# The first pair of heads in a cross-attention kernel: its key rotation on VectorE, its queries in a bank of their own, weights rounded in another order

## What is computed

```python
lat = layer_norm(latents, ln_lat_g, ln_lat_b)
ctx = layer_norm(context, ln_ctx_g, ln_ctx_b)
q = (lat @ Wq).reshape(b, n, HEADS, DHEAD).transpose(0, 2, 1, 3)
kv = ctx @ Wkv
k, v = jnp.split(kv, 2, axis=-1)
...
k = apply_rope(k, cos[None, None], sin[None, None])   # [x1*cos - x2*sin, x2*cos + x1*sin]
attn = jnp.einsum('bhnd,bhsd->bhns', q, k) * scale
attn = jnp.clip(attn, -11.0, 11.0)
attn = jax.nn.softmax(attn, axis=-1)
out = jnp.einsum('bhns,bhsd->bhnd', attn, v)
```

## Time and profile before

| what | us |
|---|---|
| median of 3 runs | 314.24 |
| all three runs | 313.40, 314.24, 314.36 |
| the profiled execution, its time | 312.95 |
| the profiled execution, its span in the trace | 311.2 |

### The profile page before, as it was taken

How to read it: one execution, slowest core, us unless ns; L and a number is a source line. 1 busy time by engine, 2 the same in 40 slices (tenths; PEclk the granted TensorE clock), 3 DMA queues, 4 the chain that set the end, 5 groups by cost and what they waited for, 6 DMA issues and landing times.

```text
span 311.2 us, 6616 instructions
## 1 busy us (share of the span) xinstructions
PE 292.3 (94%) x2482; PEld 204.0 (66%) x2482; DVE 243.4 (78%) x449; ACT 162.7 (52%) x326; POOL 209.0 (67%) x208
## 2 busy tenths in 40 slices
PE   7898999999999999999999999999999999899983
PEld 6776576666668666666687676556686665476651
DVE  3985998875875849899787798977847699687856
ACT  3446466667443734774426465774436368314741
POOL 6446775665573838686737578498827597968764
PEclk9999999999999999999999999999999999999999
DMA  7554412211210201111201111111101200000001
GB/s 218 179 151 114 123 38 57 62 36 44 60 28 9 52 17 36 35 36 36 51 19 34 37 34 36 33 38 34 36 0 37 53 1 2 0 19 0 1 2 34
DMA packets 16319, 14.24 MB, mean 46 GB/s; under 512 B 4832, under 2 KB 11808, under 8 KB 16288
## 3 DMA queue, kind: packets, MB, share of 16 engines
q1 hardware_dynamic: 14992, 13.49, 16.6%
q10 hardware_dynamic: 1296, 0.33, 0.5%
HBM read 4.89 MB, written 0.52 MB: 17 GB/s over the span
## 4 chain that ended last, share of the span: by engine, by line
PE 52%; DVE 21%; POOL 9%; issue 8%; ACT 5%; SPq 3%; DMA 2%; POOLq 0%; ACTq 0%; DVEq 0%
PE pv L645 10%; PE sc L631 9%; PE sums L666 6%; PE pj_k L569 4%; PE side L751 4%; DVE ks L1286 3%; PE pj_k L571 3%; PE pj_k L570 3%; SPq L536 3%; POOL moe L1868 3%; POOL e L1806 3%; PE side L827 2%; DVE ksin L1350 2%; DMA kswap<-ksin 2%; DVE kcos L1350 2%
## 5 line engine op out<-in xcount | busy, mean ns | idle before, releaser
L1806 POOL TENSOR_SCALAR e<-e 128x1024 f32<-128x1024 f32 x64 | 71.6, 1119 | 60.7 <-ACT e L944 47.6
L944 ACT ACTIVATE e<-sc 128x1024 f32<-128x1024 f32 x64 | 65.6, 1024 | 28.1 <-PE sc L631 28.0
L631 PEld LDWEIGHTS sc<-qs,ks 64*128 64x128 f32 x768 | 49.6, 185 | 21.7 <-issue 18.5
L645 PE MATMUL pv<-e,v 128*64 128x256 f32 x512 | 62.3, 385 | 1.6 <-POOL e L1806 0.8
L631 PE MATMUL sc<-qs,ks 64*128 64x256 f32 x768 | 62.5, 295 | 0.4 <-ACT e L944 0.2
L1799 POOL TENSOR_TENSOR krot<-kcos,kswap 128x512 f32<-128x512 f32 x32 | 45.2, 1411 | 9.8 <-DMA kswap<-ksin 7.0
L645 PEld LDWEIGHTS pv<-e,v 128*64 128x64 f32 x512 | 34.1, 136 | 24.2 <-issue 7.2
L952 ACT ACTIVATE u<-pv 128x256 f32<-128x256 f32 x32 | 12.3, 386 | 62.2 <-PE pv L645 55.5
L1286 DVE TENSOR_TENSOR ks<-krot,ks 128x512 fp32r<-128x512 f32 x32 | 33.6, 1051 | 0.1
L1350 DVE TENSOR_TENSOR ksin<-pj_k,sinT 128x512 f32<-128x512 f32 x32 | 21.9, 685 | 3.4 <-PE pj_k L571 3.2
L936 ACT ACTIVATE v<-pj_k 128x512 f32<-128x512 f32 x28 | 16.8, 598 | 14.3 <-PE pj_k L571 13.9
(11 more groups left out here) (289 smaller groups left out, 560.4 us busy)
## 6 DMA issues: line engine op xcount, KB each, us to landing
kswap<-ksin SPq DMA_DIRECT2D x126, 64.0 KB, 2.0
ctx_in<-in_ctx_dram SPq DMA_DIRECT2D x4, 256.0 KB, 3.4
prod<-in_L_xattn_Wkv_dram SPq DMA_DIRECT2D x2, 512.0 KB, 6.0
x_in<-in_x_dram SPq DMA_DIRECT2D x1, 512.0 KB, 6.0
prod<-in_L_xattn_Wq_dram SPq DMA_DIRECT2D x1, 512.0 KB, 6.8
wo<-in_L_xattn_Wo_dram SPq DMA_DIRECT2D x1, 512.0 KB, 4.4
fwe<-in_L_ffn_We_dram SPq DMA_DIRECT2D x1, 512.0 KB, 4.4
out_dram<-x_in SPq DMA_DIRECT2D x3, 128.0 KB, 1.8
```

The source lines that it names most:

```text
L631: last = nc.tensor.matmul(sc[:, h, c * NT:(c + 1) * NT], ks[rows, j % 3, k_part, chunk], qs[rows, j % 2, q_part, :], start=(k_part + q_par ...
L645: last = nc.tensor.matmul(pv_bank[DH * h:DH * h + DH, 0:NT], v[:, c, col:col + DH], e[:, j % 3, h, c, :], start=(c == 0), stop=(c == SC - 1))
L944: nc.scalar.activation(e[:, j % 3, :, 2 * half:2 * half + 2, :].rearrange("p h c n -> p h (c n)"), sc[:, :, :], ACT.Exp, scale=SCALE).then ...
L1806: nc.gpsimd.tensor_scalar(a, a, EXP_HIGH, EXP_LOW, ALU.min, ALU.max).then_inc(s_clip, 1)
```

## The change

- VectorE instead of POOL adds `krot` of pair 0, right behind the split of the transposed tokens.
- The products of pair 1 move behind that: its sines after `krot` of pair 0, its cosines after `key_lo(0)` and `query_lo(0)`.
- The queries of pair 0 go into the PSUM bank `own_bank`, and no longer take a place in `PROJECTIONS`; the places of all behind them shift by one.
- ACT rounds `wq` before it issues its two swaps, and `wv` after the transposed tokens (before: `wv`, swaps, `wq`, tokens). POOL's rest of `wv` now waits for `key_lo(0)`.
- POOL's second `affine_select` moves behind the two 1/sqrt of the start.
- ACT's `key_hi(1)` moves from slot -1 into slot 0, between the value copies and the second exponential. POOL's first clip of slot 0 moves ahead of `rotate(2)`.
- Eight `keep_busy` matmuls fewer: 5 instead of 10 ahead of the transposed tokens, 3 instead of 6 ahead of the first queries.

```diff
-WARM_UP = {"cos_T": 11, "ctx_T": 0, "sin_T": 4, "lat_T": 10, "queries": 6, "scores": 6}
+WARM_UP = {"cos_T": 11, "ctx_T": 0, "sin_T": 4, "lat_T": 5, "queries": 3, "scores": 6}
...
-        if 0 <= slot + 1 < NPAIR:
+        if 1 <= slot + 1 < NPAIR:
             units.append(("queries", slot + 1))
...
         def query_bank(j):
-            return pj_k[PLACE["queries", j] % 2]
+            return pj_k[PLACE["queries", j] % 2] if j else own_bank
...
                 if j == 0:
                     pe.wait_ge(s_wq, 1)
-                bank_free("queries", j)
+                else:
+                    bank_free("queries", j)
...
-            act.wait_ge(ld["wv"], 16)
-            nc.scalar.activation(wvS[:, 0, :], wv_in, ACT.Copy).then_inc(s_wvhi, 1)
+            act.wait_ge(ld["wq"], 16)
+            nc.scalar.activation(wqS[:, 0, :], wq_in, ACT.Copy).then_inc(s_wqhi, 1)
 
             act.wait_ge(s_kmul, 1)
             for r in (2, 3):
                 to, at = HALF * r, HALF * (r ^ 1)
                 act.dma_start(kswap[to:to + HALF, 0, :], ksin[at:at + HALF, 0, :]).then_inc(s_kswap[0], 16)
-            act.wait_ge(ld["wq"], 16)
-            nc.scalar.activation(wqS[:, 0, :], wq_in, ACT.Copy).then_inc(s_wqhi, 1)
             take("lat_T", 0)
+            act.wait_ge(ld["wv"], 16)
+            nc.scalar.activation(wvS[:, 0, :], wv_in, ACT.Copy).then_inc(s_wvhi, 1)
...
                     value_copy(1)
+                    key_hi(1)
...
-                if 0 <= slot + KV_AHEAD < NPAIR:
+
+                if 0 <= slot + KV_AHEAD < NPAIR and slot + KV_AHEAD != 1:
                     key_hi(slot + KV_AHEAD)
...
-            def key_products(j):
+            def key_products(j, which=(0, 1)):
...
-                for dst, trig in ((ksin, sinT), (kcos, cosT)):
+                for i in which:
+                    dst, trig = ((ksin, sinT), (kcos, cosT))[i]
...
             key_products(0)
-            key_products(1)
             tokens_normalise(0)
             dve.wait_ge(s_wqhi, 1)
             split_lo(wqS[:, 1, :], wq_in, wqS[:, 0, :]).then_inc(s_wq, 1)
             split_latT(0)
+
+            dve.wait_ge(s_kmul, 2)
+            dve.wait_ge(s_kswap[0], 64)
+            nc.vector.tensor_tensor(krot[:, 0, :], kcos[:, 0, :], kswap[:, 0, :], ALU.add).then_inc(s_krot, 1)
+            key_products(1, (0,))
             key_lo(0)
             query_lo(0)
+            key_products(1, (1,))
...
+            ctx_rstd(0)
+            tokens_rstd(0)
             nc.gpsimd.affine_select(out=sp_v, in_=sp_v, compare_op=ALU.not_equal, fill=-1.0, base=-1,
...
-            ctx_rstd(0)
-            tokens_rstd(0)
-
+
+
+            pool.wait_ge(s_klo, 1)
             pool.wait_ge(s_wvhi, 1)
             nc.gpsimd.tensor_tensor(wvS[:, 1, :], wv_in, f(wvS[:, 0, :]), ALU.subtract).then_inc(s_wv, 1)
...
-                if 0 <= slot + KV_AHEAD < NPAIR:
+
+                if slot == 0:
+                    clip(slot, 0)
+                if 1 <= slot + KV_AHEAD < NPAIR:
                     rotate(slot + KV_AHEAD)
                 second_layer(slot, -1)
-                if 0 <= slot < NPAIR:
+                if 1 <= slot < NPAIR:
                     clip(slot, 0)
```

## The result

The changed kernel takes 315.82 us (median of 15 runs, 314.12 to 317.24), the kernel before beside it 313.74 (15 runs): ratio 1.0057, 95% interval 1.0038 to 1.0075. It is slower by 0.6%, where no change was forecast, and it lies outside the range. The profiled execution took 316.20 us, its span is 314.4 (before: 311.2); the two traces differ by 3.2 us where the medians differ by 2.1. Medians are over all runs, while a ratio compares the means of the fast ones (without 317.30 and 317.65 of e2 and 543.88 of e7), so it need not equal the ratio of the medians.

A forecast was written before the change was run, and what follows sets the result against it. PE's losses in the first 40 us were taken to bound the kernel; 2.04 us at the scores, 0.6 left at the clips, summed to 0.45 off the median 314.24, 313.8 us, range 312.1 to 314.7.

The forecast's parts named there:

- The entry: Sums of pair 1, at 36.17, wait for VectorE's additions; what the sums win is what the kernel wins.
- Tokens and first keys: Stretch from `lat` to the first scores: scores at 18.19, 2.04 us earlier.
- The mechanism: SP's queue: later sines of pair 1 delay its swap, so the swap of pair 2 starts at 21.73 instead of 20.71.
- and from there to POOL's start 2.14: From the last issue of pair 2's swap to POOL's `krot` of pair 2: 2.14 us, as in the trace.
- rival 1: SP's queue does not stall again, swaps of pairs 2 and 3 come 0.74 earlier: 313.1 us, chance 0.25.
- rival 3: Swaps of pairs 2 and 3 land late, 3.5 instead of about 2.1: slower, 315.6 us, chance 0.15.
- some 2 us: PE's wait ahead of the first product with values, which starts near 28.9; a sign that the forecast is right.
- The `affine_select` beside `lat`: POOL beside VectorE: `lat` ends at 13.86 if held, about 13.5 if free; the middle, 13.68, was taken.
- Covered, as said: PE has 1.4 us to spare ahead of the first product with values; smaller delays ahead of it are hidden.
- the scores' lead: PE's first scores of pair 0 come 2.04 us earlier, at 18.19 instead of 20.23.
- the 0.6 us that were left at the clips: POOL's clips of pair 0 end at 28.85 instead of 29.46, leaving 0.6 of the 2.04 us.

The follow-up runs named there:

- e2: Changed kernel with the swap of pair 2 ahead of the context of batch 2 and the loads in SP's queue: 315.07 us, ratio 1.0021.
- e7: e3 with `krot` of pair 0 back on POOL: 311.76 us, ratio 0.9939.
- e3: Changed kernel with both products of pair 1 early again, ahead of `lat`: 311.68 us, ratio 0.9948.
- e6: Changed kernel with POOL's second `affine_select` back ahead of the two 1/sqrt: 314.85 us, ratio 1.0021.
- e5: Changed kernel with 10 unread matmuls in PE's wait ahead of the first product with values: 313.30 us, ratio 1.0006.
- e9: Kernel before with one edit, POOL's first clip of pair 0 ahead of `krot` of pair 2: 312.38 us, ratio 0.9958.
- e4: Kernel before with only both products of pair 1 moved behind the split of the transposed tokens: 317.72 us, ratio 1.0148.
- e10: e7 with the first clip of pair 0 behind `krot` of pair 2 again: 313.91 us, ratio 1.0007.

## Why the prediction was wrong

**Right.** *The entry.* What the sums of pair 1 lose is what the kernel loses; 275 us behind them hold in all 13 traces. *Tokens and first keys.* Scores at 18.58 against 18.19: `krot` on VectorE took 0.68 (0.69 taken), `ks` 0.69, and 0.37 of the difference is there already when the swap of pair 1 is issued (17.34 against 16.97), of which most is the later start. *The mechanism.* The later sines hold up the swap of pair 1, SP's loads slip with it, and the swap of pair 2 stands right behind the context's load, later than before.

**The step that failed is a term of the sum: "and from there to POOL's start 2.14".** The working had put `krot` of pair 2 at 26.44; it started at 28.49, 2.05 later, in three pieces. 0.37 is the difference above. From the first issue of pair 1's swap to the last of pair 2's it was 25.06 - 17.34 = 7.72 instead of 4.76 + 2.57 = 7.33, so 0.39: the long issue left the swap, as rival 1 had it, but went to `wo` (1.74 us), which stands in the same queue, and nothing was gained. The largest piece, 1.29, is the landing: from the last issue to POOL 3.43 (28.49 - 25.06) instead of 2.14. The swap's landing had been carried over from a place where the last load was issued 2.35 us ahead of it (18.36 to 20.71) to one where it is 0.12 ahead.

The last DMA of the swap took 3.3 us instead of 2.0 to land. No run changes the landing alone: e2 takes the loads away and meets another wait.

**What happened is nearest to rival 3**, which had a chance of 0.15. Its landing of 3.5 us is what the trace shows (3.3 to 3.8), its clips at 30.63 ended at 30.88, and its time of 315.6 was measured as 315.82. The prediction had named the loads that stand closer and the landing from which the case decides, 2.6 us, and still took the 2.14 us of a swap that follows them at a distance. The 3.5 of the earlier trace rows was luck: it belongs to the swap issued at 244.9 us, with no load in front of it. Rows for a better chance were there in the swap of pair 2 itself: in the kernel before its first two DMAs, 2.35 and 2.91 us behind the last load, took 2.7 and 2.8 us, its last two 2.0.

The Trainium skill has a rule that should have raised that chance: "DMA: Bandwidth & Descriptors", section "Queues, rings and completion order", says that on each DMA engine descriptors are consumed in the order of their ring, and that the write which counts up the semaphore lands only after every earlier write of that engine. The traces agree: behind loads issued 0.12, 1.18 and 2.35 us ahead the swap of pair 2 landed in 3.4, 2.9 and 2.4 us (medians of four, changed kernel, e3, before), and 2.0 with the loads behind it (e2).

**A step was missing altogether: the clock.** The prediction let PE wait "some 2 us" ahead of the product with values and priced the wait alone. The clock fell in it, and that cost another 1.2 to 1.7 us (e6, e5). Its working held none of this, and so the nearness of rival 3 to the measured time is in part luck: it put VectorE's `ks` last, and in the trace the sums follow PE without a wait; and it adds 1.33 us to a median of 314.24, where the measured rise is 2.08 from 313.74.

**Weighed wrongly.** The `affine_select` beside `lat`: the middle of held and free was taken. `lat` was held: it ended at 14.17, 0.32 behind the `affine_select` (13.85), as it had ended 0.34 behind `wvS`. So the Trainium skill's rule, "SBUF — State Buffer", section "SBUF: two separate sides", held here for a tensor-scalar operation too. By e6 its price is 0.30 us in `lat`, of which 0.16 reaches the swap.

**Covered, as said.** The rest of `wv` behind the keys (`wvS` at 18.18, 2.39 us), the own bank and the fewer unread matmuls cost nothing that can be seen. What the working did not separate is which edit wins: it credited the scores' lead with the 0.6 us that were left at the clips. In e9 the clip in POOL's idle time is worth 1.8 us by itself (1.3 by the ratio) with scores no earlier than before (20.26), and e7 shows no loss from scores 0.44 us later than in e3: the lead is worth nothing that can be measured.

## What to carry to other kernels

A duration read for a transfer belongs to what stands in front of it in its queue: when a change pushes loads closer to a small transfer on the path, take the landing from rows with as many bytes in front and as little time between, not the median. Closeness alone misleads, as the swap of pair 3 shows (0.10 us behind 132 KB, landed in 2.0). Where an estimate leaves PE waiting for about 2 us, read the granted clock behind waits of that length before pricing the wait alone. A change of many edits is best told apart by what each does to the one wait that binds: here one clip moved into idle time was the gain, and one pair's products moved out of their place cost more than twice as much.

## What the runs showed of the hardware

PE's waits of 1.87, 2.14 and 2.45 us ahead of the first product with values (e4, e6, changed kernel) each went with a fall of the clock to 0.50 (1.2 GHz); behind those of 0.84 and 1.35 us (before, e10) it stayed at 1.00. In the changed kernel and e6 it fell during the wait and stayed low for almost 7 us, though PE was busy for more than five of them; in e4 it fell a little behind the wait (the microsecond from 33 has 0.63) and was back after some 3.5. So a wait of about 2 us can cost about half as much again behind it. The length of one wait does not settle it: behind 2.21 us ahead of the second scores of e2 the clock stayed at 1.00, at the start of e5 it fell to 0.50 a little behind a wait of 1.68 us, and in three of twelve runs of e6 hardly any fall is on record.

One issue of a DMA on SP took twice its time or more close to an instruction load, whichever DMA stood there: in the kernel before the second issue of the swap (1.33 us at 21.27, with a load between 21 and 22), in the changed kernel that of `wo` (1.74 us at 19.80), in e6 that of `wo` too (1.28 at 19.25, with a load between 18.8 and 19). The row of the changed kernel's DMA packets from 19 to 20 us:

```profile
q8 instruction: 1, 0.02, 10.1%
```

Not every load does it: beside the one at 37.8 us of the kernel before no issue of the swap took more than 0.72 us. Whether the load makes the issue long, or both follow from something else, was not tried.
